# A decoder layer with routed experts on one Trainium2 core: the mean square of the second normalisation made by ScalarE squares with row sums

## The chip, the cores and the metric

The kernel runs on one core of one Trainium2 chip. The metric is the device time of one execution in microseconds (us). Each version is timed in several runs, and one further execution is recorded by the hardware profiler.

## The reference

One decoder layer over 64 sequences of 64 tokens of width 128, float32. Three sublayers follow each other, each with a layer norm ahead and a residual around it: causal self attention, cross attention to a context with a two-layer network behind it, and a block with rotary attention and eight experts, two of which are chosen for each token.

```python
x = x + self_attn(layernorm(x))
x = x + cross_attn(layernorm(x), ctx)
f = layernorm(x)                                  # third sublayer
h = f + rotary_attn(rmsnorm(f, g1))
x = x + h + moe(rmsnorm(h, g2))                   # top 2 of 8 experts
# rmsnorm(h, g) = h * rsqrt(mean(h * h, axis=-1) + 1e-6) * g
```

The change is in the mean of `h * h`, which is what the second RMS norm needs ("the second normalisation" below).

## The kernel before

**Tiles, jobs and steps.** The 4096 tokens are cut into 8 tiles of 512 tokens, each held as 4 subtiles of 128 rows by 128 columns. A job is one sublayer's attention of one tile (L136): 24 jobs, ordered so that a tile's three sublayers stand at least four jobs apart. Within a job, `walk` (L245) goes over four pairs of sequences p = 0 to 3. For each pair it runs, on every engine, the same sequence of items: the steps of place 0, `attend` of the pair before, `scores` of the pair after, `shift` of the pair after (VectorE: row maximum L1346, subtraction L1350), `exps` (TensorE: transposes of the shifted scores L1164; ScalarE: the exponentials L1209), and the steps of place 1. The steps are the projections, norms and transposes that belong to the neighbouring jobs, and the table STEPS (L144) says at which pair and place of job n the steps of jobs n-2, n-1, n+1 and n+2 run. Each engine walks this list by itself, in this order, and does its own part of each item; an instruction that waits on a semaphore holds everything behind it on its engine.

**The score loop.** TensorE writes a pair's scores to one set of PSUM banks `ps_s` (mask L1139, product L1152), so the next pair's scores wait for VectorE's subtraction L1350 (semaphore `centered`). In TensorE's own order, `attend` of the pair before (L1180), which needs ScalarE's exponentials, stands ahead of them. ScalarE's exponentials in turn stand behind whatever steps came earlier on ScalarE.

**The second normalisation.** With job n-1 a rotary one, at pair 1, place 1 of job n ("wo" and "st2" in L153): TensorE multiplies by the output weights (L1099), VectorE adds the layer-normed rows (L1427, into `hres`), then makes batch statistics of each of the four subtiles (`stats_of`, L1370) and aggregates them to mean and variance (L1375, into `mv`). GpSimd (`rms`, L1509) makes mean times mean, plus variance, plus epsilon, and the power -0.5 into `rstd`: four small steps (all at L1481). At pair 2, place 1 ("ap2") ScalarE scales the rows by `rstd` (L1244), which also waits until an older tile's rows have been moved; these rows are transposed, routed and moved to DRAM by GpSimd's indirect DMAs (L1546).

**What else stands at that place on ScalarE.** Within one place the steps of n-2 come first, then n-1, n+1 and n+2. At pair 1, place 1, that is: "st2" of n-1 (nothing for ScalarE before), "v" of n+1 when n+1 is rotary (copies of the values, L1253), and "ap" of n+2 (the rows of a layer norm, L1226, with GpSimd's factors), followed by "cT" (L1290) when n+2 is a cross job. Behind them come the exponentials of pair 2.

```python
L146  CROSS: (((), ("st",)), ((), ("ap", "cT")), ((), ("k",)), ((), ("xT",))),          # job n+2
L150  ROTARY: ((("q",), ("qr",)), ((), ("v",)), ((), ()), ((), ()))},                   # job n+1
L153  ROTARY: (((), ()), (("oT",), ("wo", "st2")), ((), ("ap2",)), ((), ("hT",)))},      # job n-1
```

Seven of the eight tiles meet "st2" inside the walk, in jobs 12, 15, 17, 19, 21, 22 and 23. The eighth does in the experts' stage, which starts at about 481 us: there 71 blocks of 128 gathered rows go through an expert each, and the last tile's remaining steps are hung behind single blocks by TAIL_AT (L196; "st2" behind block 3).

Of the kernel before, what the change touches and what calls it, by code (L numbers as in the profile page):

```python
# [25 lines left out]
ALU = mybir.AluOpType  # L26
# [253 lines left out]

def count_uses():

    uses, norms = {}, {}
    turns = [0] * BANKS

    def new(key, bank=None):
        bank = len(uses) % BANKS if bank is None else bank
        uses[key] = Use(len(uses), bank, turns[bank])
        turns[bank] += 1

    def steps(items, bank=None):
        for name, n in items:
            if name in ("st", "st2"):
                norms[name, n] = len(norms) + 1
            if name not in NOT_ON_PE:
                new((name, n), bank)

    def exps(n, p):
        for g in range(2):
            new(("tr", n, p, g))  # L300

    steps(first_steps())
    walk(steps, lambda n, p: None, lambda n, p: None, lambda n, p: new(("att", n, p)), exps)
    held = list(turns)
    for j in range(-1, FULL):
        steps(tail_steps(j), TAIL_BANK)
    return uses, norms, held


USES, NORMS, TURNS = count_uses()  # L310
THIRDS = {m: 0 for m in range(-1, len(NORMS) + 1)}
for (name, n), m in NORMS.items():
    if name == "st" and KIND_OF[n] == ROTARY:
# [14 lines left out]
def _build(nc, ctx, a, out):  # L328
    def sb(name, shape, dt=F32):
        return ctx.enter_context(nc.sbuf_tensor(name, shape, dt))  # L330

    def sem(name):
        return ctx.enter_context(nc.semaphore(name))
# [27 lines left out]
    moved = [sb(f"moved{r}", [P, 2, SUB, ROW]) for r in range(2)]  # L361
    hres = sb("hres", [P, SUB, E])
    stats = sb("stats", [P, SUB, 6])
    mv = [sb(f"mv{r}", [P, SUB, 2]) for r in range(2)]
    rstd = [sb(f"rstd{r}", [P, SUB]) for r in range(2)]
    rboth = [sb(f"rboth{r}", [P, SUB]) for r in range(2)]
# [103 lines left out]
    ring_drained = [sem(f"ring_drained{r}") for r in range(BANKS)]  # L470
    stats_ready = sem("stats_ready")
    mv_ready = sem("mv_ready")
    pool_step = sem("pool_step")
    factors_ready = sem("factors_ready")
    normed = sem("normed")
# [33 lines left out]
    def used(*key):  # L509

        return USES[key]
# [689 lines left out]
    def _(act):  # L1201
# [16 lines left out]
        def apply(n):  # L1218

            m, t, kind = NORMS["st", n], TILE_OF[n], KIND_OF[n]  # L1220
            act.wait_ge(factors_ready, m)
            r = m % 2
            for s in range(SUB):
                bias = shift[r][:, 1 if kind == ROTARY else 0, s:s + 1]
                scale = (rboth if kind == ROTARY else rstd)[r][:, s:s + 1]
                last = nc.scalar.activation(xh[:, s, :], xs[t][:, s, :], ACT.Identity, bias=bias, scale=scale)  # L1226
            last.then_inc(normed, 1)

        def apply_third(n):
# [5 lines left out]
                                            bias=shift[r][:, 0, s:s + 1], scale=rstd[r][:, s:s + 1])  # L1235
            last.then_inc(third_rows, 1)

        def apply_rms(n):

            m, t = NORMS["st2", n], TILE_OF[n]  # L1240
            act.wait_ge(factors_ready, m)
            wait(act, rows_moved[BUFFER_OF[t]], MOVED * EARLIER[t])
            for s in range(SUB):
                last = nc.scalar.activation(hn[BUFFER_OF[t]][:, s, :], hres[:, s, :], ACT.Copy, scale=rstd[m % 2][:, s:s + 1])  # L1244
            last.then_inc(normed, 1)
# [10 lines left out]
        def use(name, n):  # L1256
            kind, r = KIND_OF[n], n % 2
            if name == "ap":
                apply(n)
            elif name == "ap2":  # L1260
                apply_rms(n)
            elif name == "ap3":
                apply_third(n)
            elif name in ("lg", "rk"):
                u, t = used(name, n), TILE_OF[n]
                ps = ring[u.bank][:].rearrange("p (s e) -> p s e", e=EXPERTS)
                if name == "lg":
                    wait(act, sel_ready, t)
                    act.wait_ge(ring_filled, u.filled())
                    nc.scalar.activation(logits[:], ps[:, 0:SUB, :], ACT.Copy).then_inc(ring_drained[u.bank], 1)  # L1270
                else:
                    wait(act, rows_known, t)
                    act.wait_ge(ring_filled, u.filled())
                    rows = SUB + 1 if t in (TILES_A - 1, TILES - 1) else SUB
                    nc.scalar.activation(rank[:, 0:rows, :], ps[:, 0:rows, :], ACT.Copy)\
                      .then_inc(ring_drained[u.bank], 1)
# [63 lines left out]
    def _(dve):  # L1340
# [24 lines left out]

        def stats_of(m, src):

            wait(dve, mv_ready, m - 1)
            for s in range(SUB):
                last = V.bn_stats(stats[:, s, :], src[:, s, :])  # L1370
            last.then_inc(stats_ready, 1)
            wait(dve, factors_ready, m - 2)
            dve.wait_ge(stats_ready, m)
            for s in range(SUB):
                last = V.bn_aggr(mv[m % 2][:, s, :], stats[:, s, :])  # L1375
            last.then_inc(mv_ready, 1)

        def table(c):
# [5 lines left out]
        def use(name, n):  # L1384
            kind, t = KIND_OF[n], TILE_OF[n]
            if name == "st":
# [3 lines left out]
                    u = used("wo" if kind == CROSS else "ff", JOB_OF[t, kind - 1])  # L1390
                    dve.wait_ge(ring_drained[u.bank], u.drained())
                stats_of(NORMS["st", n], xs[t])
            elif name == "st2":
                u = used("wo", n)
                dve.wait_ge(ring_drained[u.bank], u.drained())
                stats_of(NORMS["st2", n], hres)
            elif name == "c0":
                choose_dve(dve, n)
            elif name == "c1":
# [66 lines left out]
    def _(pool):  # L1466
# [19 lines left out]
                pool.sem_inc(last, 1)  # L1486

        def layer_norm(m, both):
            r = m % 2
            var, mean = mv[r][:, :, 1], mv[r][:, :, 0]  # L1490
            pool.wait_ge(mv_ready, m)
            wait(pool, normed, m - 2)
            wait(pool, third_rows, THIRDS[m - 2])
            step(pt[:, 0, :], var, eps5, ALU.add)
            step(rstd[r][:], pt[:, 0, :], neg_half, ALU.pow)
            step(pt[:, 3, :], mean, rstd[r][:], ALU.mult)
            if both:


                step(shift[r][:, 0, :], zero, pt[:, 3, :], ALU.subtract)  # L1500
                step(pt[:, 1, :], pt[:, 0, :], eps6, ALU.mult)
                step(pt[:, 2, :], pt[:, 1, :], var, ALU.add)
                step(rboth[r][:], pt[:, 2, :], neg_half, ALU.pow)
                step(pt[:, 3, :], mean, rboth[r][:], ALU.mult)
                step(shift[r][:, 1, :], zero, pt[:, 3, :], ALU.subtract, factors_ready)
            else:
                step(shift[r][:, 0, :], zero, pt[:, 3, :], ALU.subtract, factors_ready)

        def rms(m):  # L1509
            r = m % 2  # L1510
            var, mean = mv[r][:, :, 1], mv[r][:, :, 0]
            pool.wait_ge(mv_ready, m)
            wait(pool, normed, m - 2)
            wait(pool, third_rows, THIRDS[m - 2])
            step(pt[:, 0, :], mean, mean, ALU.mult)
            step(pt[:, 1, :], pt[:, 0, :], var, ALU.add)
            step(pt[:, 2, :], pt[:, 1, :], eps6, ALU.add)
            step(rstd[r][:], pt[:, 2, :], neg_half, ALU.pow, factors_ready)

        def use(name, n):  # L1520
            kind, t, r = KIND_OF[n], TILE_OF[n], n % 2
            if name == "st":
                layer_norm(NORMS["st", n], kind == ROTARY)
            elif name == "st2":
                rms(NORMS["st2", n])
            elif name == "ap" and kind == CROSS:
                pool.wait_ge(normed, NORMS["st", n])
                G.tensor_tensor(xs[t], xs[t], b2[:].unsqueeze(1).broadcast_to([P, SUB, E]),
# [80 lines left out]
```

## Time and profile before

| | us |
|---|---|
| median of 3 runs | 657.97 (657.83 to 663.3) |
| profiled execution, own time | 664.7 |
| its span in the trace | 662.8 |
| walk over the 24 jobs and what lies ahead of it | up to about 480.9 |
| experts and the end | about 480.9 to 662.8 |

Times in the timelines are us from the start of the span. A row of the timeline gives the start, the time covered, engine, line, operation, tile written and tiles read with shapes, and how many instructions were merged; in brackets stands how long the engine had been idle before and what ended that. PE is TensorE, DVE is VectorE, ACT is ScalarE, POOL is GpSimd.

### The profile page before, as it was taken

To read this page: it belongs to the slowest core of one execution; us is meant where nothing else is said; L and a number is where in the kernel's file an instruction comes from. 1 tells how busy PE (TensorE), PEld (TensorE's weight loads), DVE (VectorE), ACT (ScalarE), POOL (GpSimd) and SP (SyncE) were. 2 spreads that over 40 slices of the span, in tenths; PEclk is the share of its full clock that TensorE was granted. 3 is DMA by queue.
4 is the path that set the end of the run, shared out by engine and by line. 5 is a ranking of instruction groups with operands and counts; after the bars stand their busy time and mean duration, and the time that the engine had idled before them with its cause. 6 is when DMAs were issued, how large, how long until landed. Compare 5 with 4: busy or idle time off the path is not lost.

```text
span 662.8 us, 29824 instructions
## 1 busy us (share of the span) xinstructions
PE 592.8 (89%) x12373; PEld 463.3 (70%) x12373; DVE 471.2 (71%) x1134; ACT 380.8 (57%) x758; POOL 262.9 (40%) x370
## 2 busy tenths in 40 slices
PE   4699899999999989899999989898689999999990
PEld 2366666666676666567766756565489998999990
DVE  4278688787878788778898989769936673333462
ACT  3355466666665666467667456534367666776750
POOL 6000101010122133246256465744516777754551
PEclk9699899999999999699999989987879999999995
DMA  4400911010100101001011000100023222432445
GB/s 127 135 20 20 297 47 37 3 48 3 47 3 19 37 13 31 26 15 60 4 43 35 31 31 19 34 32 11 27 69 85 65 78 73 110 98 62 140 144 170
DMA packets 44963, 38.97 MB, mean 59 GB/s; under 512 B 11248, under 2 KB 37424, under 8 KB 44832
## 3 DMA queue, kind: packets, MB, share of 16 engines
q1 hardware_dynamic: 36432, 24.22, 12.5%
q0 software_dynamic: 4320, 8.92, 4.1%
q10 hardware_dynamic: 4080, 3.93, 1.8%
q8 instruction: 101, 1.65, 1.1%
q14 instruction: 30, 0.25, 0.1%
HBM read 18.75 MB, written 12.01 MB: 46 GB/s over the span
## 4 chain that ended last, share of the span: by engine, by line
PE 63%; DVE 20%; issue 7%; POOL 4%; ACT 3%; DMA 2%; SPq 0%; POOLq 0%; ACTq 0%; DVEq 0%
PE ps_s L796 14%; PE ring L1164 9%; PE ring L1126 7%; PE ps_s L1152 7%; DVE rmax L1346 6%; PE ring L804 6%; PE ring L1180 5%; DVE shifted L1350 5%; PE ring L1040 3%; PE ps_s L1139 2%; PE ring L1049 2%; PE ring L1106 2%; DVE stats L1370 2%; ACT xh L1226 2%; PE ring L1102 2%
## 5 line engine op out<-in xcount | busy, mean ns | idle before, releaser
L1209 ACT ACTIVATE probsT<-ring 128x512 f32<-128x512 f32 x192 | 104.9, 594 | 141.7 <-PE ring L1164 141.5
L1346 DVE TENSOR_REDUCE rmax<-ps_s 128x16 f32<-128x1024 f32 x96 | 117.2, 1221 | 36.8 <-PE ps_s L1152 36.1
L1350 DVE TENSOR_TENSOR shifted<-ps_s,rmax 128x1024 f32<-128x1024 f32 x96 | 117.6, 1225 | 9.9
L1164 PEld LDWEIGHTS ring<-const,shifted 128*128 128x128 f32 x768 | 87.9, 147 | 47.2 <-issue 43.1
L1164 PE MATMUL ring<-const,shifted 128*128 128x128 f32 x768 | 112.1, 291 | 7.7 <-DVE shifted L1350 3.5
L1180 PEld LDWEIGHTS ring<-vbd,probsT 128*32 128x32 f32 x6144 | 64.2, 111 | 45.4 <-issue 29.1
L887 DVE TENSOR_TENSOR room<-room,ps_s 128x384 f32<-128x384 f32 x71 | 39.3, 554 | 79.0 <-PE ring L804 60.7
L760 POOL DMA_INDIRECT y_dram<-room x71 | 70.4, 992 | 60.0 <-DVE room L892 47.8
L796 PE MATMUL ps_s<-room 128*128 128x128 f32 x648 | 83.2, 279 | 1.3 <-issue 0.8
L1180 PE MATMUL ring<-vbd,probsT 128*32 128x18 f32 x6144 | 73.7, 188 | 10.8 <-issue 7.2
L796 PEld LDWEIGHTS ps_s<-room 128*128 128x128 f32 x648 | 78.5, 196 | 2.0 <-issue 1.2
L1546 POOL DMA_INDIRECT moved_dram<-moved,pos_i x56 | 55.9, 998 | 58.4 <-PE ps_s L1152 37.1
L1481 POOL TENSOR_TENSOR pt<-mv,small 128x4 f32<-128x4 f32 x24 | 4.8, 202 | 180.5 <-DVE mv L1375 180.5
L1152 PE MATMUL ps_s<-room,qT 32*64 32x256 f32 x1536 | 70.8, 416 | 4.2 <-issue 2.4
L804 PE MATMUL ring<-w_exp,room 128*128 x426 | 59.1, 275 | 0.5 <-DVE room L892 0.5
L838 ACT ACTIVATE room<-w_exp 128x768 f32 x54 | 45.3, 843 | 18.7 <-issue 18.2
L804 PEld LDWEIGHTS ring<-w_exp,room 128*128 128x128 f32 x426 | 53.2, 192 | 0.7 <-issue 0.7
L1253 ACT ACTIVATE vbd<-ring 64x512 f32<-64x512 f32 x48 | 30.4, 634 | 17.5 <-PE ring L1049 17.2
L1360 DVE RECIPROCAL rden<-ring 128x16 f32<-128x16 f32 x96 | 23.9, 249 | 22.8 <-PE ring L1180 22.2
L850 ACT ACTIVATE room<-ps_s 128x384 f32<-128x384 f32 x71 | 33.7, 474 | 5.2 <-PE ps_s L796 5.2
L1481 POOL TENSOR_TENSOR rstd<-pt,small 128x4 f32<-128x4 f32 x32 | 33.2, 1036 | 2.5
L1152 PEld LDWEIGHTS ps_s<-room,qT 32*64 32x64 f32 x1536 | 23.7, 134 | 14.8 <-issue 4.7
(186 smaller groups left out, 933.3 us busy)
## 6 DMA issues: line engine op xcount, KB each, us to landing
room<-kS SPq DMA_DIRECT2D x96, 64.0 KB
room<-moved_dram SPq DMA_DIRECT2D x71, 65.0 KB, 1.8
room<-y_dram ACTq DMA_DIRECT2D x10, 256.0 KB, 3.1
room<-in_x SPq DMA_DIRECT2D x8, 256.0 KB, 4.3
cin<-in_ctx SPq DMA_DIRECT2D x8, 192.0 KB, 3.3
w_exp<-in_L_ffn_wg SPq DMA_DIRECT2D x1, 1536.0 KB, 8.1
w_exp<-in_L_ffn_wu SPq DMA_DIRECT2D x1, 1536.0 KB, 11.8
w_exp<-in_L_ffn_wd SPq DMA_DIRECT2D x3, 512.0 KB, 12.2
```

What stands on the lines that cost most here:

```text
L760: G.indirect_dma_start(out=y_dram, in_=yb[r], in_offset=None, out_offset=bass.IndirectOffsetOnAxis(ap=xb[r].bitcast(I32)[:, E:E + 1], axis ...
L796: last = mm(bank[r][:, k * P:(k + 1) * P], w, xbT[r], start=True, stop=True)
L804: last = mm(y_bank[r], hh[r][:, k * P:(k + 1) * P], weights(e, W_DOWN + k * E, E), start=(k == 0), stop=(k == HC - 1))
L838: nc.scalar.activation(w_held[c % HELD], w, ACT.Copy).then_inc(w_copied, 1)
L1126: last = mm(ps_g[:], w, (cT if kind == CROSS and name == "k" else xT)[:], start=True, stop=True)
L1152: last = mm(ps_s[SEQ * b:SEQ * b + SEQ, g], qT[r][some, tok:tok + SEQ], kbd[r][some, :, tok:tok + SEQ], start=not causal, stop=True)
L1164: last = nc.tensor.transpose(ring[u.bank][:, k * P:(k + 1) * P], flat[:, c:c + P], ident)
L1180: last = mm(ring[u.bank][rows, c:c + 2 * (D + 1)], probsT[p % 2][:, k, rows], vbd[r][:, at:at + 2 * (D + 1)], start=True, stop=True)
L1209: nc.scalar.activation(probsT[p % 2][:, 4 * g:4 * g + 4, :], ring[u.bank][:].rearrange("p (k c) -> p k c", c=P), ACT.Exp, scale=SCALE)\
L1346: V.reduce_max(rmax[p % 2][:].rearrange("p (g k) -> p g k", g=GROUPS), ps_s, AX.X).then_inc(rmax_ready, 1)
L1350: V.tensor_tensor(shifted[p % 2][:].rearrange("p (g k) s -> p g k s", g=GROUPS), ps_s, rmax[p % 2][:].rearrange("p (g k) -> p g k", g=GROU ...
L1546: G.indirect_dma_start(out=moved_dram, in_=moved[b][:, k, s, :], in_offset=None, out_offset=bass.IndirectOffsetOnAxis(ap=pos_i[b][:, k, s: ...
```

## The change

For the second normalisation alone, VectorE's batch statistics and aggregation go. ScalarE gets a new function `sum_squares` at the step "st2", with four squares (one for each subtile), each with the row sum of its result in `mean_square`. GpSimd's `rms` now adds epsilon to that and takes the power: two steps for four. The layer norms keep their batch statistics; as `mv` now serves them alone, its two buffers are counted by layer norms (LAYERS), and VectorE's waits with them.

```diff
+        def sum_squares(n):
+            t, u = TILE_OF[n], used("wo", n)
+            act.wait_ge(ring_drained[u.bank], u.drained())
+            if t >= 2:
+                act.wait_ge(factors_ready, NORMS["st2", JOB_OF[t - 2, ROTARY]])
+            for s in range(SUB):
+                last = nc.scalar.activation(squared[:, t % 2, s, :], hres[:, s, :], ACT.Square, scale=float(E) ** -0.5,
+                                            accum_out=mean_square[t % 2][:, s:s + 1])
+            last.then_inc(squares_ready, 1)
...
             if name == "ap":
                 apply(n)
+            elif name == "st2":
+                sum_squares(n)
...
         def stats_of(m, src):
-            wait(dve, mv_ready, m - 1)
+            turn = LAYERS.index(m)
+            wait(dve, mv_ready, turn)
...
-            wait(dve, factors_ready, m - 2)
-            dve.wait_ge(stats_ready, m)
+            if turn >= 2:
+                dve.wait_ge(factors_ready, LAYERS[turn - 2])
+            dve.wait_ge(stats_ready, turn + 1)
...
-            elif name == "st2":
-                u = used("wo", n)
-                dve.wait_ge(ring_drained[u.bank], u.drained())
-                stats_of(NORMS["st2", n], hres)
...
-        def rms(m):
+        def rms(m, t):
             r = m % 2
-            var, mean = mv[r][:, :, 1], mv[r][:, :, 0]
-            pool.wait_ge(mv_ready, m)
+            pool.wait_ge(squares_ready, t + 1)
...
-            step(pt[:, 0, :], mean, mean, ALU.mult)
-            step(pt[:, 1, :], pt[:, 0, :], var, ALU.add)
-            step(pt[:, 2, :], pt[:, 1, :], eps6, ALU.add)
-            step(rstd[r][:], pt[:, 2, :], neg_half, ALU.pow, factors_ready)
+            step(pt[:, 0, :], mean_square[t % 2][:], eps6, ALU.add)
+            step(rstd[r][:], pt[:, 0, :], neg_half, ALU.pow, factors_ready)
```

`ring_drained` of the bank of "wo" is what VectorE's addition L1427 counts up.

## Rows read from the trace of the kernel before

**Rows 1.** The page's chain that ended last: shares of the span by line.

```profile
PE ps_s L796 14%; PE ring L1164 9%; PE ring L1126 7%; PE ps_s L1152 7%; DVE rmax L1346 6%; PE ring L804 6%; PE ring L1180 5%; DVE shifted L1350 5%; PE ring L1040 3%; PE ps_s L1139 2%; PE ring L1049 2%; PE ring L1106 2%; DVE stats L1370 2%; ACT xh L1226 2%; PE ring L1102 2%
```

**Rows 2.** Groups by line and shape: count, busy us, mean ns, idle before.

```profile
L1370 DVE BATCH_NORM_STATS2 stats<-hres 128x6 f32<-128x128 f32 x32 | 7.0, 281 | 0.2
L1375 DVE BATCH_NORM_AGGREGATE mv<-stats 128x2 f32<-128x6 f32 x128 | 12.2, 157 | 3.2
...
L844 ACT ACTIVATE room<-ring 128x128 f32<-128x128 f32 x71 | 19.6, 276 | 18.8 <-PE ring L786 16.6 <-DMA y_dram<-room 1.3
L1244 ACT ACTIVATE moved<-hres,rstd 128x128 f32<-128x128 f32 x28 | 9.0, 391 | 11.9 <-DMA moved_dram<-moved,pos_i 6.1 <-POOLq L1486 5.8
L1330 ACT ACTIVATE bias_qk<-ps_s 128x2 f32<-128x2 f32 x1 | 0.2, 172 | 0.1
L850 ACT ACT_TABLE_LOAD x1 | 1.3, 1283 | 0.0
...
L1481 POOL TENSOR_TENSOR pt<-mv 128x4 f32<-128x4 f32 x8 | 1.7, 212 | 14.2 <-DVE mv L1375 12.3 <-ACT xh L1226 1.8
```

**Rows 3.** Timeline of job 15 (tile 1's second normalisation), 304 to 311 us.

```profile
304.94 1.28 ACT L1253 ACTIVATE vbd<-ring 64x512 f32<-64x512 f32 x2 [1.28 <-PE ring L1049]
...
305.60 0.68 DVE L1427 TENSOR_TENSOR hres<-ring,fres 128x512 f32<-128x512 f32 x1
...
306.25 1.65 ACT L1226 ACTIVATE xh<-room,shift,rstd 128x128 f32<-128x128 f32 x4
...
307.92 0.59 ACT L1290 ACTIVATE cT<-ring 96x512 f32<-96x512 f32 x1
...
308.42 1.07 ACT L1209 ACTIVATE probsT<-ring 128x512 f32<-128x512 f32 x2
...
309.69 0.74 PE L1180 MATMUL ring<-vbd,probsT 128*32 128x18 f32 x64
...
310.65 0.33 PE L1139 MATMUL ps_s<-maskb,identb 32*32 32x256 bf16 x16 [0.23 <-DVE shifted L1350]
```

**Rows 4.** Timeline of job 12 (tile 0), 244 to 250 us.

```profile
244.00 0.68 DVE L1427 TENSOR_TENSOR hres<-ring,fres 128x512 f32<-128x512 f32 x1
...
244.47 1.65 ACT L1226 ACTIVATE xh<-room,shift,rboth 128x128 f32<-128x128 f32 x4 [1.28 <-POOLq L1486]
...
249.06 0.69 PE L1152 MATMUL ps_s<-room,qT 32*64 32x256 f32 x16 [1.14 <-DVE shifted L1350]
```

**Rows 5.** Timeline of job 17 (tile 2), 343 to 349 us.

```profile
343.27 0.68 DVE L1427 TENSOR_TENSOR hres<-ring,fres 128x512 f32<-128x512 f32 x1
...
343.67 1.65 ACT L1226 ACTIVATE xh<-room,shift,rstd 128x128 f32<-128x128 f32 x4
...
348.32 0.33 PE L1139 MATMUL ps_s<-maskb,identb 32*32 32x256 bf16 x16 [0.47 <-DVE shifted L1350]
```

**Rows 6.** Timeline of job 19 (tile 3), 381 to 388 us.

```profile
381.37 0.68 DVE L1427 TENSOR_TENSOR hres<-ring,fres 128x512 f32<-128x512 f32 x1
...
382.77 1.65 ACT L1226 ACTIVATE xh<-room,shift,rboth 128x128 f32<-128x128 f32 x4 [0.84 <-POOLq L1486]
...
386.80 1.16 PE L1152 MATMUL ps_s<-room,qT 32*64 32x256 f32 x16
```

**Rows 7.** Timeline of job 21 (tile 4), 422 to 432 us.

```profile
422.93 0.68 DVE L1427 TENSOR_TENSOR hres<-ring,fres 128x512 f32<-128x512 f32 x1
...
424.44 1.65 ACT L1226 ACTIVATE xh<-room,shift,rboth 128x128 f32<-128x128 f32 x4 [0.37 <-POOLq L1486]
...
430.96 1.01 PE L1152 MATMUL ps_s<-room,qT 32*64 32x256 f32 x2 [2.04 <-issue]
```

**Rows 8.** Timeline of jobs 22 and 23 (tiles 5 and 6), two rows.

```profile
455.75 0.21 DVE L568 TENSOR_TENSOR at_expert<-chosen,rank 128x64 f32<-128x64 f32 x1
...
478.51 1.28 ACT L1244 ACTIVATE moved<-hres,rstd 128x128 f32<-128x128 f32 x4 [6.07 <-DMA moved_dram<-moved,pos_i]
```

**Rows 9.** Windows: length; busy PE, PEld, DVE, ACT, POOL; PEclk; DMA share; GB/s.

```profile
381.00:386.00 5.00, 3.02 (x103) 2.09 (x95) 4.72 (x14) 3.65 (x8) 3.58 (x9) 1.00 0.05 17
386.00:389.50 3.50, 3.46 (x81) 2.37 (x70) 2.23 (x5) 2.17 (x6) 2.56 (x3) 0.53 0.08 24
```

More of the change, by code:

```diff
@@ L281, in count_uses @@
 def count_uses():
-    uses, norms = {}, {}
+    uses, norms, layers = {}, {}, []
     turns = [0] * BANKS
@@ L294, in steps @@
                 norms[name, n] = len(norms) + 1
+            if name == "st":
+                layers.append(norms[name, n])
             if name not in NOT_ON_PE:
@@ L306, in count_uses @@
         steps(tail_steps(j), TAIL_BANK)
-    return uses, norms, held
-USES, NORMS, TURNS = count_uses()
+    return uses, norms, layers, held
+USES, NORMS, LAYERS, TURNS = count_uses()
 THIRDS = {m: 0 for m in range(-1, len(NORMS) + 1)}
@@ L363, in _build @@
     stats = sb("stats", [P, SUB, 6])
+    squared = sb("squared", [P, 2, SUB, E])
+    mean_square = [sb(f"mean_square{r}", [P, SUB]) for r in range(2)]
     mv = [sb(f"mv{r}", [P, SUB, 2]) for r in range(2)]
@@ L472, in _build @@
     mv_ready = sem("mv_ready")
+    squares_ready = sem("squares_ready")
     pool_step = sem("pool_step")
@@ L1371, in stats_of @@
             last.then_inc(stats_ready, 1)
-            wait(dve, factors_ready, m - 2)
-            dve.wait_ge(stats_ready, m)
+            if turn >= 2:
+                dve.wait_ge(factors_ready, LAYERS[turn - 2])
+            dve.wait_ge(stats_ready, turn + 1)
             for s in range(SUB):
-                last = V.bn_aggr(mv[m % 2][:, s, :], stats[:, s, :])
+                last = V.bn_aggr(mv[turn % 2][:, s, :], stats[:, s, :])
             last.then_inc(mv_ready, 1)
@@ L1488, in layer_norm @@
         def layer_norm(m, both):
-            r = m % 2
-            var, mean = mv[r][:, :, 1], mv[r][:, :, 0]
-            pool.wait_ge(mv_ready, m)
+            r, turn = m % 2, LAYERS.index(m)
+            var, mean = mv[turn % 2][:, :, 1], mv[turn % 2][:, :, 0]
+            pool.wait_ge(mv_ready, turn + 1)
             wait(pool, normed, m - 2)
@@ L1507, in layer_norm @@
                 step(shift[r][:, 0, :], zero, pt[:, 3, :], ALU.subtract, factors_ready)
-        def rms(m):
+        def rms(m, t):
             r = m % 2
-            var, mean = mv[r][:, :, 1], mv[r][:, :, 0]
-            pool.wait_ge(mv_ready, m)
+            pool.wait_ge(squares_ready, t + 1)
             wait(pool, normed, m - 2)
             wait(pool, third_rows, THIRDS[m - 2])
-            step(pt[:, 0, :], mean, mean, ALU.mult)
-            step(pt[:, 1, :], pt[:, 0, :], var, ALU.add)
-            step(pt[:, 2, :], pt[:, 1, :], eps6, ALU.add)
-            step(rstd[r][:], pt[:, 2, :], neg_half, ALU.pow, factors_ready)
+            step(pt[:, 0, :], mean_square[t % 2][:], eps6, ALU.add)
+            step(rstd[r][:], pt[:, 0, :], neg_half, ALU.pow, factors_ready)
         def use(name, n):
@@ L1524, in use @@
             elif name == "st2":
-                rms(NORMS["st2", n])
+                rms(NORMS["st2", n], t)
             elif name == "ap" and kind == CROSS:
```

## The prediction

> **What bounds the kernel now.** I began with the chain of waits that ended last [rows 1]. It is mostly TensorE lines, but the score loop's two VectorE lines (the row maximum L1346 and the subtraction L1350) stand in it, the batch statistics L1370 with 2% of the span, and ScalarE's layer norm rows L1226 with another 2%. So VectorE's statistics cost time. They are for 24 layer norms and 8 second normalisations, though, and only the 8 go. A share of the chain does not say what is next in line, so I then read the timeline around each place where a second normalisation meets the walk. The reader is to follow one ScalarE queue there, in job 15 [rows 3]: the values copy at 304.94, the layer norm rows at 306.25, `cT` at 307.92 and the exponentials at 308.42 run almost without a gap, and TensorE's `attend` starts at 309.69, as soon as the exponentials end (308.42 + 1.07 = 309.49). `attend` ends at 310.43; the next scores start at 310.65, having waited 0.23 us for VectorE's subtraction. So at this very place two chains arrive within 0.23 us of each other: VectorE's, which the change shortens, and ScalarE's, which it lengthens.
>
> **What is removed.** On VectorE 4 statistics of 281 ns and 4 aggregations of 157 ns per tile [rows 2], back to back some 1.25 us with what lies between them (they overlap a little, and one semaphore wait stands between the two fours). On GpSimd two of four steps, each 0.21 us and a hand-over, some 0.5 us per tile. In the walk there are seven tiles, so the ceiling of the gain is 7 x 1.25 = 8.8 us, if nothing else were near. But the next scores also stand behind `attend` in TensorE's order, so what a tile can give is no more than the time TensorE waited for the subtraction after `attend`: 1.14 us in job 12 [rows 4], 0.23 in job 15 [rows 3], 0.47 in job 17 [rows 5], and nothing in jobs 19 and 21, where no such wait is printed [rows 6, 7]. That is 1.84 us over five tiles, before ScalarE pays anything.
>
> **What is added: the price S of four squares.** No instruction with a row sum is in the trace. Nearest rows: a 128x128 copy takes 276 ns, the four scalings of L1244 391 ns each, and a tiny activation 172 ns [rows 2]. Low end: the four squares run as the copy does and overlap, 1.0 us. High end: each is a copy plus a small instruction that fetches the sum, one behind the other, 4 x (276 + 172) = 1.8, with hand-overs 2.0 us. I take S = 1.6, nearer the high end, since the sum has to get out of the engine somehow; the four layer norm rows in a row, which carry two pointers, cover 1.65 [rows 3].
>
> The Trainium skill (ScalarE: Activation LUTs, What ACT_TABLE_LOAD costs) gives an activation with immediate operands 186 ns + 0.833 ns per element, so 293 ns for 128; the copy's 276 agrees, and by it alone four squares would be 1.17 us; it gives no price for reading a sum.
>
> **What is added: a wait.** This is the larger part. `sum_squares` waits for VectorE's addition L1427, and on ScalarE it stands ahead of the values copy of n+1, the rows of n+2 and the exponentials of pair 2. Before, none of these waited for the addition. So with the addition's end (start + 0.68) plus 0.06 of hand-over as the start of the squares, the layer norm rows L1226 start later by:
> - job 12: 244.74 + S against 244.47, 0.27 + S = 1.87 [rows 4]
> - job 15: the values copy, 1.28, also falls behind the squares: 306.34 + S + 1.28 against 306.25, 1.37 + S = 2.97 [rows 3]
> - job 17, the same: 344.01 + S + 1.28 against 343.67, 1.62 + S = 3.22 [rows 5]
> - job 19: 382.11 + S + 1.28 against 382.77, 0.62 + S = 2.22 [rows 6]
> - job 21: 423.67 + S + 1.28 against 424.44, 0.51 + S = 2.11 [rows 7]
>
> In every one of these the exponentials follow the rows directly, so they slip by the same, and so does `attend`, and behind it in TensorE's order the next scores. What TensorE waited for the subtraction is slack for this, and goes off: 1.87 - 1.14 = 0.73; 2.97 - 0.23 = 2.74; 3.22 - 0.47 = 2.75; 2.22; 2.11. Sum 10.55 us. VectorE's subtraction, now 1.25 us earlier, finds `attend` late and wins nothing. I count these delays in full: behind them the score loop has no stock of finished work, as each pair's scores need the pair before to be subtracted.
>
> The other places. In job 22 there is no layer norm to follow; the squares delay the values copy and with it a ring bank, but the next row maximum stood behind the placing of rows, which began at 455.75 [rows 8], and the rank copy it needs comes out at about the same time: 0, at most 0.4 us. In job 23 nothing waits behind; there the scaling waited 6.07 us for a move of an older tile's rows [rows 8], whose last DMAs stand behind `rms` in GpSimd's queue. From the addition's end the squares take 1.6 us for the statistics' 1.25, and `rms` is then 0.5 us shorter: a gain of some 0.15 us. In the experts' stage the squares add 1.6 us to ScalarE behind block 3, where ScalarE works a block ahead: 0 to 1 us, taken 0.2. Together 0.
>
> VectorE's waits on `factors_ready` for its buffers now name layer norms alone, at least as old as before; no cost.
>
> **Two second-order terms.** When TensorE idled ahead of job 19's scores (3.02 us busy in 381 to 386), the granted clock was 0.53 behind it, nearly all of the stretch at the lower level of 1.2 GHz [rows 9], and the score product took 1.16 us for 0.69 in job 12 [rows 6, 4]. With 2 to 3 us more idle, jobs 12, 15 and 17 may fall in the same way: from 0 to 3 x 1.4 us (mask and transposes too), taken as two products and their masks, +1.1. In the other direction, TensorE in job 21 stood 2.04 us within the next scores with nothing the trace shows to wait for [rows 7]. If that is a delivery of instructions that goes on while TensorE waits for `attend`, the 2.1 us of this job vanish in it: 0 to -2, taken -1. Net 0.
>
> **Sum.** +10.5 us. The profiled execution should go from 664.7 to about 675.2. That execution lies 6.7 above the median of the runs; the difference carried to the median gives 657.97 + 10.5 = 668.5 us.
>
> **The rivals.**
> - VectorE is the bound and the relief counts: 8.8 us, 649.2 us. For it: L1370 is on the chain [rows 1]. Against: it needs `attend` not to be the next in line, and the waits in rows 3 to 7 let at most 1.84 us through, even with ScalarE unhurt. The deciding point is where the exponentials end against the subtraction; it turns only if ScalarE's delay stays below TensorE's wait, that is 0.23 to 1.14 us, in most jobs. Chance 0.04.
> - The delay is real but mostly taken up: S at 1.0 (5 x 0.6 = 3.0 less), job 21's stall swallows its delay (a further 1.5 at that S), and jobs 12 and 19 recover half of theirs (0.9): 10.5 - 5.4 = +5.1, 663.1 us, within 1%. For it: the stall of 2.04 us and the low-clock stretch already paid in job 19. Against: nothing in jobs 15 and 17, which hold half of the sum. Chance 0.16.
> - The squares need another activation table: one load took 1283 ns [rows 2], and there and back would be 2.57 us a tile, in five tiles 12.8 us more, 681.3 us. For it: the trace has only two loads, at the first exponential and at the first Silu, and no square. Against: copies, Identity and Relu run beside the exponentials with no load between. Chance 0.05. The Trainium skill (ScalarE: Activation LUTs, Table sets: the hidden batching unit) says that cheap functions such as copy and relu are in every set; it does not name the square there, and would price a switch at about 2.66 us with its drain.
>
> **How the numbers follow.** My forecast has a chance of 0.75. Its own range comes from S (1.0 to 2.0, five tiles: -3 to +2), the clock (-1.1 to +3.1) and job 21's stall (-1 to +1): the ends do not meet often, so about 663 to 674. The second rival pulls the low end to 661 and the table a little beyond the top, 675. About 1% (6.6 us) is what a measurement of this kernel can tell from no change: slower by more than that 0.80 (forecast and table), within 0.16, faster 0.04.
>
> **What would show it.** Right: in the profile after, the squares in job 15 begin at the end of L1427 and the values copy, L1226 and the exponentials follow them without a gap; `attend` has idle time ahead of it, released by ScalarE's exponentials, 2 to 3 us in jobs 15, 17, 19 and 21; the wait for the subtraction ahead of the next scores is gone. Four squares cover 1.0 to 2.0 us. The clock falls behind those idles. Wrong: if scores still start on the subtraction and come earlier than before, VectorE was the bound; if table loads stand around the squares, the third rival; if the idle is there but the job after takes it back, the delays are not additive.

## The result, and the profile after

The changed kernel took 675.69 us in the median of 6 runs (670.28 to 679.49), the kernel before 661.14 in 6 runs beside it. The ratio is 1.0209, 95% interval 1.017 to 1.0248: 13.8 us slower on 661 (11.2 to 16.4). Some runs of a kernel are over 1.5% longer than its fastest, at a lower granted clock; they are left out of the ratios and of the fit below. The forecast was slower by 10.5 us, to 668.5 in the median, with a range of 661 to 675. It started from a median of 657.97 in three runs; on that, the ratio gives 671.7, while the measured 675.69 lies just above the top of the range. The profiled execution went from 664.7 to 675.53 (forecast: 675.2), its span from 662.8 to 673.6.

The chain that ended last of the changed kernel, the fifteen lines with the largest shares (to compare with [rows 1]; L1346 and L1350 are now L1364 and L1368, L1226 is L1231, the moves L1546 are L1559):

```profile
PE ps_s L801 12%; PE ring L1169 8%; PE ring L1131 8%; PE ps_s L1157 7%; PE ring L1185 6%; PE ring L809 6%; DVE rmax L1364 6%; DVE shifted L1368 4%; PE ring L1045 4%; PE ps_s L1144 2%; PE ring L1111 2%; PE ring L1054 2%; ACT xh L1231 2%; POOL moved_dram L1559 2%; PE ring L1107 2%
```

The page shows the largest shares only. L1370 (L1389 now) and the squares (L1250) stand below them: followed in order of time, the chain still holds the layer norms' statistics, and it has taken in the squares in all seven jobs, 8.6 us in all. At job 15 it ran through VectorE before (first three rows) and runs through ScalarE now (the last four): start, time, engine, tile and line.

```profile
306.31 0.88 DVE stats L1370 x4
...
309.37 1.24 DVE shifted L1350
...
310.65 0.33 PE ps_s L1139 x16
```

```profile
306.70 0.69 DVE hres L1443
...
307.41 1.28 ACT squared L1250 x8
...
311.55 0.60 ACT cT L1308
...
312.29 1.10 PE ring L1131 x2
```

So the chain names the new path at the place itself, and the shares by line hide it. The groups of the changed kernel, by line and shape (count, busy us, mean ns, idle before and releaser), answer to [rows 2]:

```profile
L1250 ACT ACTIVATE squared<-hres 128x128 f32<-128x128 f32 x32 | 9.5, 297 | 19.2 <-DVE hres L1443 19.2
...
L1250 ACT ACTIVATION_READ_ACCUMULATOR squared<-hres 128x1 f32 x32 | 6.0, 187 | 0.0
...
L1331 ACT ACT_TABLE_LOAD x1 | 1.3, 1283 | 0.7 <-PEq L1613 0.7
L855 ACT ACT_TABLE_LOAD x1 | 1.3, 1283 | 0.0
```

Each square is a 297 ns activation and a 187 ns instruction that reads the sum. The idle column is the one to look at: 19.2 us in which ScalarE did nothing until VectorE's addition (L1443, L1427 before) had ended. There are still two table loads. Now job 15, the timeline that answers to [rows 3]:

```profile
306.70 0.68 DVE L1443 TENSOR_TENSOR hres<-ring,fres 128x512 f32<-128x512 f32 x1
...
307.41 0.31 ACT L1250 ACTIVATE squared<-hres 128x128 f32<-128x128 f32 x1 [2.70 <-DVE hres L1443]
...
308.60 1.26 ACT L1269 ACTIVATE vbd<-ring 64x512 f32<-64x512 f32 x2
...
309.88 1.65 ACT L1231 ACTIVATE xh<-room,shift,rstd 128x128 f32<-128x128 f32 x4
...
309.91 0.66 PE L1169 MATMUL ring<-const,shifted 128*128 128x128 f32 x4 [1.22 <-ACT vbd L1269]
311.55 0.59 ACT L1308 ACTIVATE cT<-ring 96x512 f32<-96x512 f32 x1
...
312.05 1.07 ACT L1214 ACTIVATE probsT<-ring 128x512 f32<-128x512 f32 x2
...
312.29 1.10 PE L1131 MATMUL ring<-cT,w_xqk 96*128 96x512 f32 x2 [1.72 <-ACT cT L1308]
...
313.32 0.88 PE L1185 MATMUL ring<-vbd,probsT 128*32 128x18 f32 x64
...
314.50 1.16 PE L1157 MATMUL ps_s<-room,qT 32*64 32x256 f32 x16
```

Read down ScalarE's rows: it idles 2.70 us until the addition, the four squares take from 307.41 to 308.60, 1.19 us, and the values copy, the layer norm rows, the context copy and the exponentials follow without a gap, as in [rows 3], only later. From the addition's start to the layer norm rows it is 3.18 us now and was 0.65. TensorE twice stands for ScalarE (1.22 and 1.72 us). Its scores no longer wait for the subtraction. And the score product itself takes 1.16 us, which in [rows 4] takes 0.69: the clock has fallen. One row each that shows the same in jobs 12, 17, 19 and 21, and the scaling in job 23 (timelines of the changed kernel):

```profile
247.83 0.66 PE L1045 MATMUL ring<-const,xh 128*128 128x128 f32 x4 [1.48 <-ACT xh L1231]
...
353.37 1.10 PE L1131 MATMUL ring<-cT,w_xqk 96*128 96x512 f32 x2 [1.73 <-ACT cT L1308]
...
394.64 0.66 PE L1045 MATMUL ring<-const,xh 128*128 128x128 f32 x4 [3.03 <-ACT xh L1231]
...
437.71 0.66 PE L1045 MATMUL ring<-const,xh 128*128 128x128 f32 x4 [1.81 <-ACT xh L1231]
...
442.62 1.00 PE L1157 MATMUL ps_s<-room,qT 32*64 32x256 f32 x2 [1.82 <-issue]
...
489.56 1.28 ACT L1260 ACTIVATE moved<-hres,rstd 128x128 f32<-128x128 f32 x4 [6.36 <-DMA moved_dram<-moved,pos_i]
```

The two profiles start their jobs at different times, so the fair measure is the interval from one addition into `hres` to the next. Four of them hold jobs 15, 17, 19 and 21. Windows of the kernel before (columns as in [rows 9]):

```profile
305.60:343.27 37.67, 36.42 (x960) 26.19 (x949) 33.79 (x91) 25.25 (x51) 17.58 (x27) 1.00 0.09 30
343.27:381.37 38.10, 36.62 (x936) 26.07 (x926) 34.03 (x91) 23.98 (x50) 22.24 (x34) 1.00 0.10 31
381.37:422.93 41.56, 39.33 (x923) 27.21 (x925) 36.65 (x95) 22.83 (x49) 25.52 (x39) 0.96 0.09 31
422.93:450.82 27.89, 24.25 (x573) 16.10 (x562) 19.86 (x50) 13.16 (x28) 12.32 (x16) 0.88 0.07 24
```

and of the changed kernel:

```profile
306.70:347.78 41.08, 37.70 (x908) 26.78 (x899) 32.79 (x82) 26.14 (x58) 17.14 (x25) 0.96 0.09 27
347.78:389.76 41.98, 37.75 (x968) 26.89 (x968) 32.87 (x83) 25.28 (x57) 21.76 (x32) 0.96 0.09 28
389.76:432.83 43.07, 39.12 (x918) 27.07 (x922) 35.50 (x87) 24.27 (x57) 25.18 (x37) 0.96 0.09 30
432.83:461.39 28.56, 23.50 (x579) 15.72 (x566) 18.75 (x42) 13.09 (x34) 11.80 (x14) 0.88 0.07 23
```

They grew by 3.41, 3.88, 1.51 and 0.67 us, together 9.47 of the span's 10.8. (The rest: 0.24 ahead of job 12, 0.86 in its interval, 0.08 in job 22's, 1.25 in job 23's, and 1.10 less behind it.) VectorE's busy time fell in each, and the granted clock fell from 1.00 to 0.96 in the first two.

### The profile page after: what moved, and what is told of

It is laid out like the page before. It is cut to its first block, busy times and chain, and to the rows that moved or that the text cites. A ratio compares the mean times of both kernels' runs of the same rounds, so it can differ in the third digit from the quotient of the medians.

```text
span 673.6 us, 29798 instructions
## 1 busy us (share of the span) xinstructions
PE 594.1 (88%) x12373; PEld 464.1 (69%) x12373; DVE 462.3 (69%) x1070; ACT 388.9 (58%) x822; POOL 259.0 (38%) x354
## 3 DMA queue, kind: packets, MB, share of 16 engines
q0 software_dynamic: 4320, 8.92, 4.0%
q8 instruction: 101, 1.65, 1.1%
## 4 chain that ended last, share of the span: by engine, by line
PE 61%; DVE 17%; issue 8%; ACT 5%; DMA 4%; POOL 4%; SPq 1%; POOLq 0%; ACTq 0%; DVEq 0%
PE ps_s L801 12%; PE ring L1169 8%; PE ring L1131 8%; PE ps_s L1157 7%; PE ring L1185 6%; PE ring L809 6%; DVE rmax L1364 6%; DVE shifted L1368 4%; PE ring L1045 4%; PE ps_s L1144 2%; PE ring L1111 2%; PE ring L1054 2%; ACT xh L1231 2%; POOL moved_dram L1559 2%; PE ring L1107 2%
## 5 line engine op out<-in xcount | busy, mean ns | idle before, releaser
L1364 DVE TENSOR_REDUCE rmax<-ps_s 128x16 f32<-128x1024 f32 x96 | 117.3, 1221 | 35.7 <-PE ps_s L1157 35.1
L1368 DVE TENSOR_TENSOR shifted<-ps_s,rmax 128x1024 f32<-128x1024 f32 x96 | 117.6, 1225 | 10.2 <-DVE rmax L1364 0.5
L1559 POOL DMA_INDIRECT moved_dram<-moved,pos_i x56 | 55.7, 995 | 63.6 <-PE ps_s L1157 43.2
```

The costliest lines, as they stand in the source:

```text
L1364: V.reduce_max(rmax[p % 2][:].rearrange("p (g k) -> p g k", g=GROUPS), ps_s, AX.X).then_inc(rmax_ready, 1)
L1368: V.tensor_tensor(shifted[p % 2][:].rearrange("p (g k) s -> p g k s", g=GROUPS), ps_s, rmax[p % 2][:].rearrange("p (g k) -> p g k", g=GROU ...
L1559: G.indirect_dma_start(out=moved_dram, in_=moved[b][:, k, s, :], in_offset=None, out_offset=bass.IndirectOffsetOnAxis(ap=pos_i[b][:, k, s: ...
```

## The experiments

Theory of the queue: ScalarE's order holds back the exponentials and with them TensorE's `attend` and the next scores. Its rivals: the squares' own time is the cost; VectorE's relief counts; and, after the first runs, the clock. Ratios are to the kernel before, run beside each on the same chip; 1% is 6.6 us.

| kernel | ratio | interval |
|---|---|---|
| the change | 1.0209 | 1.017 to 1.0248 |
| e1, wait alone | 1.0183 | 1.0142 to 1.0223 |
| e2, squares alone | 1.0028 | 0.9991 to 1.0065 |
| e3, statistics kept | 1.0222 | 1.0185 to 1.0259 |
| e4, squares behind | 1.0075 | 1.0046 to 1.0105 |
| e5, a pair later | 1.0031 | 0.9995 to 1.0067 |
| e6, eight squares | 1.0356 | 1.031 to 1.0403 |
| e7, change filled | 1.0017 | 0.9976 to 1.0058 |
| e8, wait alone filled | 0.9978 | 0.9948 to 1.0009 |
| e9, kernel before filled | 0.9971 | 0.9937 to 1.0005 |
| e10, change, small products | 1.0101 | 1.0065 to 1.0136 |
| e11, wait alone, small products | 1.0001 | 0.9969 to 1.0034 |

**The wait alone (e1)**, on the kernel before:

```diff
+            elif name == "st2":
+                act.wait_ge(ring_drained[used("wo", n).bank], used("wo", n).drained())
```

Expected: 

> The kernel before, statistics on VectorE as they were, but ScalarE waits at the step of the second normalisation for VectorE's addition, and does nothing more there. Theory of the queue (the cost is ScalarE's order: values copy, layer norm rows and exponentials held until the addition has ended): by the formula of the prediction with S = 0, job 15 +1.1 us, job 17 +1.2, job 19 +0.6, job 21 +0.5, job 12 nothing: +3.4 us over the kernel before, 0.5%. Theory of the price (the squares' own time is the cost): no change, 0.

Measured: ratio 1.0183, 12 us (9.4 to 14.7). No square, no relief of VectorE, and most of the loss is there. The price theory, which gave 0, falls. But the queue's formula gave 3.4, far less than the 12. Its timeline in job 15:

```profile
306.39 1.28 ACT L1253 ACTIVATE vbd<-ring 64x512 f32<-64x512 f32 x2 [2.70 <-DVE hres L1429]
...
310.10 1.96 PE L1126 MATMUL ring<-cT,w_xqk 96*128 96x512 f32 x2 [1.72 <-ACT cT L1292]
...
313.35 1.16 PE L1152 MATMUL ps_s<-room,qT 32*64 32x256 f32 x16
```

ScalarE idles for the addition as in the changed kernel, and behind TensorE's 1.72 us of waiting the projection takes 1.96 us (1.10 in the changed kernel) and the score product 1.16: the lower clock level. That made the clock the next suspect.

**The squares alone (e2)**: the kernel before, with four squares of the constant identity tile at the step "st2" of ScalarE, no wait, no reader.

Expected: 

> The kernel before, statistics on VectorE as they were, with four squares with row sums at the same place of ScalarE's queue, of a constant tile, so that they wait for nothing and nobody waits for them. Theory of the queue: they run in the time in which ScalarE waited there anyway, and only what does not fit comes out: with four squares at 1.2 us, as the trace of the changed kernel shows, job 15 +1.0, job 17 +0.7, job 21 +0.8, job 19 +0.35, job 12 nothing: +2.9 us, 0.4%. Theory of the price: all or most of the changed kernel's growth in the profiles, +8 to +11 us.

Measured: 1.0028, +1.8 us (-0.6 to +4.3). The queue's 2.9 lies within the interval, and so does 0; 8 to 11 does not. The traces speak for 0: the four intervals that held jobs 15, 17, 19 and 21 are 37.67, 38.07, 40.49 and 22.74 us at full clock, 0.2 us in all above those of e9 below, which has no squares and the full clock too. The same instructions at the same place cost little where nothing makes them wait.

**Statistics kept (e3)**: the changed kernel with L1370 and L1375 made for `hres` as before, into tiles without a reader.

Expected: 

> The changed kernel, in which VectorE makes the old statistics and aggregations of the second normalisation as well, into tiles that nobody reads. Theory of the queue: TensorE's attend comes 2 us or more after VectorE is free, so VectorE's relief is worth nothing and taking it back costs nothing: within 1 us of the changed kernel in jobs 12 to 21, some 1 us more at most from jobs 22 and 23. Theory that the relief counts in part: +1.8 to +8.8 us over the changed kernel.

Measured: 1.0222 against 1.0209, that is 0.9 us more (2.7 less to 4.5 more). The times rule out that the relief counts in full (8.8), not that 2 or 3 us of it count. In job 15 VectorE's extra aggregation and TensorE's `attend`:

```profile
305.85 0.38 DVE L1425 BATCH_NORM_AGGREGATE mv_dead<-stats_dead 128x2 f32<-128x6 f32 x4
...
311.70 0.26 DVE L1381 RECIPROCAL rden<-ring 128x16 f32<-128x16 f32 x1 [2.54 <-PE ring L1188]
```

VectorE makes the statistics and still idles 2.54 us for `attend` (L1188): what the change took off VectorE is not on the path here. In e3's chain in order of time the extra statistics stand in none of the seven jobs, the squares in all.

**Squares behind (e4)**: on ScalarE alone, the step "st2" goes behind the others of its place.

```diff
         def steps(items):
-            for name, n in items:
+            for name, n in sorted(items, key=lambda x: x[0] == "st2"):
                 use(name, n)
```

Expected: 

> The changed kernel, with the squares moved on ScalarE alone behind the values copy, the layer norm rows and the context copy of the same place, so that the addition has ended when ScalarE comes to them; all other engines keep their order. Theory of the queue: only the squares' 1.2 us are left, less TensorE's slack: jobs 12, 15, 17, 19, 21 +0.1, 1.0, 0.7, 1.2, 1.2, together +4.2 us over the kernel before, that is 6 to 7 us less than the changed kernel in the profile. Theory of the price: as the changed kernel.

Measured: 1.0075, +5.0 us (3.0 to 6.9). Nearly two thirds of the loss go with the order of one queue; the 4.2 lies in the interval. In its trace the squares still wait for the addition in jobs 22 and 23 alone, 4.5 us for the change's 19.2.

**A pair later (e5)**: "st2" to pair 2, "ap2" to pair 3, "hT" to pair 0 of the next job in the table of steps.

Expected: 

> The changed kernel, with the second normalisation's steps put one pair later in the table of steps: squares at pair 2, place 1, scaling of the rows at pair 3, place 1, their transposes at pair 0, place 0 of the next job. At pair 2 the squares stand where the scaling stood (1.2 us for 1.3), the addition is long done, and GpSimd's two steps have a whole pair's time. Theory of the queue: the growth goes, and VectorE's relief may show where TensorE waited for the subtraction (1.84 us over three jobs); against it stands that in pair 3 the scaling (1.3) takes the place of the transposed rows' copy (0.6) beside third rows and an expert's weights: from -2 to +2 us against the kernel before, best guess 0. Theory of the price: 8 us or more over the kernel before.

Measured: 1.0031, +2.0 us (-0.3 to +4.4): no difference from the kernel before can be told, as expected, and no gain. The loss goes where the wait is gone. What VectorE's relief is worth there is not shown, as the moved steps can cost something too (job 15's interval is 39.52 us, at full clock, for 37.67 before).

**Eight squares (e6)**: the four squares twice.

Expected: 

> The changed kernel with the four squares made twice, the first four into a sum that nobody reads. Theory of the queue: in jobs 12, 15, 17, 19 and 21 no slack is left behind the squares, so each microsecond more is a microsecond of the kernel: 5 x 1.2 = +6 us over the changed kernel, job 22 and 23 up to 1.2 more each. Theory that only the wait counts and squares run beside other limits: 0 to 1 us.

Measured: 1.0356, that is 0.0147 or 9.7 us above the change, with an interval of 5.7 to 13.7. The queue gave 6, and up to 2.4 more from jobs 22 and 23; the wait theory's 0 to 1 falls. In the traces the four intervals grow by 5.9 us over the change and job 22's by 1.2. So once the queue stands at the addition, squares are paid in full. Whether something more comes on top here cannot be told from the noise.

**What comes on top.** Each run's result lists its mean granted clock, as a share of 2.4 GHz. The 77 runs of the kernel before that count took 660.8 us at 0.954 on average; with two levels that is 2 x (1 - 0.954) x 660.8 = 61 us at 1.2 GHz. A straight line through these runs gives 0.33 us more for each us at the lower level (correlation 0.79). The change ran at 0.9435, 76 us; the wait alone at 0.9438, 75; eight squares at 0.9348, 89. By the line that is 5, 5 and 9 us of their 14, 12 and 24. The squares alone ran at 0.954. The two profiles do not show this part: both ran at 0.946, 72 and 73 us at the lower level, as the kernel before was caught in one of its longer executions. A line is no proof, so TensorE's gaps were filled.

**The change, filled (e7)**, the wait alone filled (e8) and the kernel before filled (e9): transposes of the identity tile into a free bank, which nobody reads. For e7, behind the named half of pair 2's transposes:

```diff
+                fill = {(12, 1): 10, (15, 0): 8, (15, 1): 12, (17, 0): 7, (17, 1): 12, (19, 1): 21, (21, 1): 12}.get((n, g), 0) if p == 2 else 0
+                if fill:
+                    later_bank = used("att", n, p)
+                    free(later_bank)
+                    for i in range(fill):
+                        nc.tensor.transpose(ring[later_bank.bank][:, i % 4 * P:(i % 4 + 1) * P], ident, ident)
```

Expected of e7: 

> The changed kernel, with TensorE transposing a constant tile into a free ring bank in the time in which it waited for ScalarE: at pair 2 of jobs 12, 15, 17, 19 and 21, 7 to 21 transposes of 0.14 us in each gap (1.0 to 2.9 us, a little less than the gap in the trace). Nothing reads them. Theory that the delay has two parts (ScalarE's queue, some 8 us, and the granted clock that falls behind TensorE's idle, some 6 us by the runs' mean clock and 0.35 to 0.38 us for each us at the lower level): the clock stays up in the jobs that were filled, the intervals of jobs 15 and 17 lose 1 to 1.5 us each, the mean granted clock comes back towards that of the kernel before, and the time falls by 3 to 6 us against the changed kernel. Theory of the queue alone (the lower clock is a companion that costs nothing): no change, or slower by the transposes.

Expected of e8: 

> The kernel before with the wait alone, filled in the same way: 1, 12, 12, 13 and 4 transposes at pair 2 of jobs 12, 15, 17, 19 and 21. Two parts: the wait alone cost 3.4 us by the queue and the rest of its 10 to 12 by the clock, so filled it should stand 3 to 6 us above the kernel before, 5 us or more below the wait alone. Queue alone, or a cost of the wait that is neither: as the wait alone, 10 to 12 us above the kernel before.

Expected of e9: 

> The kernel before, without any part of the change, with such transposes in three of its own gaps: 7 behind pair 2 of job 19, 10 ahead of the scores of job 23, 22 ahead of the last pair's transposes. If the clock behind an idle costs, two to three stretches of 3.4 us at the lower level go, each worth some 1.2 us: 2 to 4 us faster than the kernel before. If it costs nothing on the chain: no change.

Measured: e7 1.0017, 12.7 us below the change (0.0192 of 661), more than the 3 to 6 expected; e8 0.9978, 13.6 us below the wait alone, and not the 3 to 6 above the kernel before; e9 0.9971, 1.9 us below the kernel before (4.2 below to 0.3 above), no difference that can be told. The same four intervals, e7:

```profile
305.77:346.46 40.69, 38.98 (x950) 28.20 (x942) 33.01 (x82) 26.14 (x58) 17.14 (x25) 1.00 0.09 28
346.46:386.36 39.90, 38.85 (x981) 28.38 (x968) 32.93 (x83) 25.21 (x57) 21.80 (x32) 1.00 0.09 30
386.36:428.17 41.81, 40.06 (x944) 28.48 (x946) 35.40 (x87) 24.27 (x57) 25.20 (x37) 1.00 0.09 30
428.17:452.04 23.87, 21.54 (x588) 15.51 (x575) 18.64 (x43) 12.86 (x34) 11.81 (x14) 1.00 0.09 28
```

and e9:

```profile
305.93:343.59 37.66, 36.43 (x961) 26.20 (x951) 33.79 (x91) 25.27 (x51) 17.56 (x27) 1.00 0.10 30
343.59:381.48 37.89, 36.60 (x936) 26.06 (x924) 33.93 (x90) 23.97 (x50) 22.20 (x34) 1.00 0.10 31
381.48:421.96 40.48, 38.86 (x941) 27.02 (x943) 36.58 (x94) 22.71 (x49) 25.48 (x39) 1.00 0.10 32
421.96:444.72 22.76, 20.91 (x563) 14.38 (x551) 19.96 (x51) 12.74 (x28) 12.30 (x16) 1.00 0.09 29
```

All eight stand at the full clock, so this pair shows the queue nearly alone: the change costs 3.03, 2.01, 1.33 and 1.11 us, together 7.5 (1.1 of the 3.03 are two waits of e7 that no row explains). That is one trace of each. By the times, e7 stands 3.0 us above e9, with an interval of 0.5 below to 6.5 above. The mean granted clock came back as well: 0.960 in e7, 0.955 in e8 and 0.962 in e9.

The clock theory had a flaw, though. The last interval fell from 28.56 to 23.87 with 12 transposes, and the wait of 1.82 us with no visible cause was gone, in e8 and e9 too, though in e9 nothing was filled in job 21. The filled programs are longer on TensorE, and that alone may have moved it. Length is not all that decides: the wait is in the profiles of before, the change, e1, e3, e4 and e5 (1.60 to 2.15 us), shorter in e6, and absent from that of e2, whose TensorE program is as long as before. The row of e6:

```profile
447.17 1.01 PE L1158 MATMUL ps_s<-room,qT 32*64 32x256 f32 x2 [0.80 <-issue]
```

**Small products (e10, e11)**: small products in place of the transposes, as many at the same places, each of 18 columns, so that the gaps stay.

```diff
-                        nc.tensor.transpose(ring[later_bank.bank][:, i % 4 * P:(i % 4 + 1) * P], ident, ident)
+                        mm(ring[later_bank.bank][0:QUARTER, 0:2 * (D + 1)], ident[:, 0:QUARTER], ident[:, 0:2 * (D + 1)],
+                           start=True, stop=True)
```

Expected of e10: 

> The changed kernel with as many extra TensorE instructions at the same places as the filled one, so that its program is as long, but each a small product of 32 columns of weights with 18 columns, as attend's are (0.012 us each in attend's rows), so that the gaps stay open. It separates two readings of the filled kernel's gain of 10 us: the clock held up, or a TensorE program that is 164 instructions longer, in which the 2 us without any visible wait behind job 21 (in the profiles before, after, with the wait alone, with the statistics kept, with squares behind and a pair later) is gone. If the clock was the gain: lower-level stretches come back in jobs 15, 17 and 19 as in the changed kernel, and it stands 4 us or more above the filled one. If the program's length was: it is as fast as the filled one, 1 to 4 us above the kernel before. Both may hold; then job 21's interval falls to 23 to 24 us and the other three stay as in the changed kernel.

Expected of e11: 

> The wait alone, with the same small products for its 42 transposes. Clock: 3 us or more above the filled wait, with a lower-level stretch in job 15 or 17 and in job 19. Length of the program: as the filled wait, at the kernel before.

Measured: e10 1.0101, between the change and e7, 5.6 us above the filled kernel. Its four intervals:

```profile
303.34:343.10 39.76, 38.09 (x992) 27.58 (x981) 32.80 (x82) 26.05 (x58) 17.15 (x25) 1.00 0.09 29
343.10:383.06 39.96, 38.15 (x974) 27.48 (x964) 32.95 (x82) 25.21 (x57) 21.82 (x32) 1.00 0.09 30
383.06:427.72 44.66, 42.13 (x972) 29.70 (x975) 35.52 (x86) 24.52 (x57) 25.21 (x37) 0.92 0.09 29
427.72:454.26 26.54, 23.72 (x592) 16.87 (x579) 18.75 (x43) 13.09 (x34) 11.82 (x14) 0.87 0.08 26
```

The gaps did not stay. Twelve small products are 24 records here and cover 0.93 us, 0.04 a record where 0.012 were expected; twelve transposes cover 1.47. The brackets show what was left of the wait ahead of the context product in job 15, 1.72 us in the change:

```profile
308.93 1.10 PE L1131 MATMUL ring<-cT,w_xqk 96*128 96x512 f32 x2 [0.86 <-ACT cT L1315]
```

In job 19, 3.03 us became 1.60; in job 21, 1.81 became 1.71. And TensorE's program is longer than the filled one, not as long: 164 products and 164 weight loads for 82 and 82. So e10 is a kernel with its gaps about half filled, and no test of the program's length.

It does show a price of the clock. In jobs 19 and 21 ScalarE releases TensorE at the same time as in e7, 4.9 us behind the addition, and from there on the clock differs: 0.92 and 0.87 over the interval against 1.00. The row of `attend` and the score product behind it in job 21, first e7, then e10:

```profile
434.21 0.77 PE L1191 MATMUL ring<-vbd,probsT 128*32 128x18 f32 x64 [0.50 <-issue]
...
435.17 0.69 PE L1157 MATMUL ps_s<-room,qT 32*64 32x256 f32 x16
```

```profile
433.76 1.06 PE L1192 MATMUL ring<-vbd,probsT 128*32 128x18 f32 x64 [0.47 <-issue]
...
435.12 1.16 PE L1157 MATMUL ps_s<-room,qT 32*64 32x256 f32 x16
```

The two intervals are 2.85 and 2.67 us longer than filled, together 5.5, beside 5.6 in the times (2.0 to 9.2). So the clock is a cost of its own. In jobs 15 and 17, half filled, it stayed up, against the expectation. From the change to e10 there are some 7 us; the clock of jobs 15 and 17, the wait behind job 21, which is gone, and the longer program are all in it, and no run parts them.

For the wait alone the small products did as much as the transposes (e11 1.0001, e8 0.9978, intervals overlapping). The expected 3 us of the clock were not seen, but the clock did not fall either. The same four intervals, us at the granted clock:

| | job 15 | job 17 | job 19 | job 21 |
|---|---|---|---|---|
| e1, wait alone | 41.37 at 0.92 | 40.18 at 1.00 | 41.99 at 0.96 | 25.11 at 1.00 |
| e8, filled | 38.80 at 1.00 | 38.94 at 1.00 | 40.63 at 1.00 | 22.87 at 1.00 |
| e11, small products | 38.82 at 1.00 | 38.97 at 1.00 | 40.63 at 1.00 | 22.92 at 1.00 |

At full clock the wait alone costs 2.5 us (e8 against e9), where the formula gave 3.4. What e1 has over e8 is 3.9 us in the two intervals with the lower clock and 3.5 us in the two without, where its trace has waits that no row explains: 0.79 and 0.76 us in job 17 and 1.88 in job 21, all absent from e8 and e11. So most of e1's 12 us is not the delay itself: by one trace of each kernel it is the clock and these waits, about half each. Why extra instructions take the waits away is not shown.

## Why the prediction was right, and what was off

- **Direction and mechanism.** Right. ScalarE waits for the addition, what stood behind it slips, `attend` and the next scores slip with it, and VectorE's relief wins nothing: shown by the chain through the squares, by e1 (the wait alone: 1.0183), by e4 (order alone: 1.0209 to 1.0075) and by e3 (relief taken back: no change that can be told, and off the chain). The sign that was asked for came a step earlier: TensorE does not idle for the exponentials ahead of `attend` but for the values copy, the layer norm rows and the context copy, 2.94, 2.85, 3.03 and 1.81 us in jobs 15, 17, 19 and 21. The wait for the subtraction is gone, as predicted.
- **The delays job by job.** From the addition's start, the layer norm rows of job 15 come 3.18 us later now and 0.65 before: 2.53 of slip. The formula 1.37 + S gives 2.56 with the measured S. Counted from the addition, the next score product starts 0.52, 2.48, 2.53, 1.97 and 1.65 us later in jobs 12, 15, 17, 19 and 21, together 9.2, some of it the lower clock. The prediction had 10.55; its formula with S = 1.19 gives 0.32 + 2.33 + 2.34 + 1.81 + 1.70 = 8.5. The four without job 12 are 8.2 of that; e7 against e9, at full clock on both sides, show 7.5 in the traces and 3.0 (-0.5 to 6.5) in the times.
- **The price S.** Mis-sized: 1.6 taken, 1.19 measured (307.41 to 308.60). The square, with its reading of the sum, starts a new pair every 0.30 us, since the two overlap. Five jobs: 2.0 us too much. By the Trainium skill (ScalarE: Activation LUTs, What ACT_TABLE_LOAD costs) an activation with immediate operands takes 186 ns and 0.833 ns for each element, an estimate of 293 ns for 128; the trace's 297 agrees, and four of them without the reading come to 1.17.
- **The second-order terms, taken as net zero.** This was the larger error. The clock was taken at +1.1; the runs' mean clock puts it at about 5 us, and e10 against e7 show 5.6 for gaps half filled against filled. With the gaps filled, 12.7 of the 13.8 us are gone (9.0 to 16.5), the wait behind job 21 among them, so what came on top of the delays weighs at least as much as the delays themselves. The stall behind job 21 was to swallow part of that job's delay; it stayed (1.82 us for the 2.04 of [rows 7]); with eight squares, where `attend` came another 1.2 us later, it was 0.80. The two errors of opposite sign, S and the clock, left the sum at 10.5 for 13.8: the direction was reasoned, but that the size came this near was in part luck. So was 675.53 beside the forecast 675.2, since both profiles ran at the same mean clock.
- **Jobs 22 and 23.** Job 22's interval is 18.85 us for 18.77, as forecast. In job 23 the gain of 0.15 did not come: the scaling starts 9.32 us after the addition, 8.92 before [rows 8]; it waits for the moves' DMAs in both. GpSimd issued the last of these 0.9 us earlier, counted from the addition, and yet the scaling was released 0.4 us later; why is not shown. Job 23's interval grew by 1.25 us, and what comes behind it shrank by 1.10.
- **The rivals.** The table switch fell: two loads before and after. "VectorE is the bound" fell with the slower result and with e3. "Mostly taken up" did not occur.

What stays open: what the wait behind job 21 is, which no row explains and which is absent from all five profiles with a longer TensorE program (e7 to e11) and from one without (e2), with one trace of each kernel; how much of the 7 to 12 us that the small products gave back is the clock in the half-filled gaps, how much these waits and how much the length of the program; and whether the delay itself costs nearer 3 or 7.5 us.

## What to carry to other kernels

Before work is moved to an engine with time to spare, look at its queue at the very place: what stands behind the moved step, what it newly waits for, and who waits for that. The price of the moved instructions mattered less here than the wait they brought (e2 against e1), and moving them three places down the same queue took back nearly two thirds of the loss (e4). Read the chain in order of time at the place of the change, not only its shares by line. Where TensorE is left idle, look at the granted clock behind the gap and count it as a cost of its own.

## What was not expected of the hardware

- Runs of one kernel spread with the granted clock: the 77 runs of the kernel before that count lie between 656.3 and 667.0 us, with 49 to 72 us at the lower level.
- A few extra TensorE instructions nobody reads made a kernel faster: the change with 82 small products 1.0101 for 1.0209, the wait alone with 42 of them 1.0001 for 1.0183. Twelve of them, of 18 columns each, cover 0.93 us.
- Reading the row sum is an instruction of its own, 187 ns for one column, and it is hidden beside the next square: pairs of 297 and 187 ns start every 0.30 us.
